# Edge and source scatters counted anew over the stages of a four-layer graph network, and one wait less for GpSimd's gathers

## The reference

```python
# layer 0, feed-forward: a shared expert and 2 of 8 routed experts
shared = gelu(x @ W1s + b1s) @ W2s + b2s
mask = ... top-2 of softmax(x @ Wr) ...
h = gelu(einsum('bsd,edf->bsef', x, W1p) + b1p)
priv = einsum('bsef,efd->bsed', h, W2p) + b2p
x = x + shared + einsum('bsed,bse->bsd', priv, mask)
# layer 1, graph: needs the 50000 x 256 edge attributes, summed by dst
msg = relu(x[src] + edge_attr)
agg = zeros_like(x).at[dst].add(msg)
# then an MLP with normalizations, then 1 of 32 experts
# layer 2, graph: needs maxima and sums by src
m = segment_max(e, src); denom = segment_sum(exp(e - m[src]), src)
```

## Time and profile before

| | |
|---|---|
| median of 3 runs | 5876.17 us (5872.45 to 5876.91) |
| profiled execution | 5874.7 us |
| its span | 5872.7 us, mean granted TensorE clock 0.832 |
| busy share | PE 76%, PEld 50%, DVE 62%, ACT 31%, POOL 61% |
| DMA | 901.08 MB, mean 153 GB/s |
| GpSimd's edge stores (L879) | 391, some 0.99 us each |
| GpSimd's source stores (L803) | 391, 384.8 us in total, mean 984 ns |

### The profile page before, as it was taken

One profiled execution on the slowest core, in us unless ns is written; L12 is line 12 of the kernel. 1 busy time (PEld: TensorE's weight loads), 2 busy tenths in 40 slices (PEclk: granted clock), 3 DMA queues, 4 the chain that ended last, 5 costly groups with the idle time before them and its releaser, 6 DMA issues. The chain is left out here.

```text
span 5872.7 us, 84688 instructions
## 1 busy us (share of the span) xinstructions
PE 4469.9 (76%) x19486; PEld 2920.1 (50%) x19486; DVE 3651.1 (62%) x12388; ACT 1837.0 (31%) x6462; POOL 3579.9 (61%) x3819
## 2 busy tenths in 40 slices
PE   4668777778867777659488866888597688878868
PEld 3333335767843334434355535666495333346636
DVE  9987643301037775533466677888524688888875
ACT  0000002222323333212423334554143455544421
POOL 3767775676657775575577756776124477756620
PEclk9985667989976567655899988999697799999978
DMA  1053336687757675023254447987374488854400
GB/s 54 25 165 102 104 105 167 218 263 240 248 153 208 206 205 127 25 77 99 68 134 126 127 87 245 286 285 230 122 211 134 131 230 233 231 139 139 144 20 22
DMA packets 526942, 901.08 MB, mean 153 GB/s; under 512 B 101137, under 2 KB 383712, under 8 KB 518016
## 3 DMA queue, kind: packets, MB, share of 16 engines
q0 software_dynamic: 164160, 449.94, 27.7%
q1 hardware_dynamic: 301866, 317.09, 17.4%
q10 hardware_dynamic: 60438, 128.64, 7.1%
HBM read 725.55 MB, written 169.76 MB: 152 GB/s over the span
## 5 line engine op out<-in xcount | busy, mean ns | idle before, releaser
L1021 PE MATMUL bank<-small 128*125 128x256 f32 x1660 | 818.7, 615 | 277.8 <-DVE small L988 173.0
L969 POOL DMA_INDIRECT small<-tabA,idxD x830 | 803.2, 968 | 275.2 <-issue 181.3
L1021 PEld LDWEIGHTS bank<-small 128*125 128x125 f32 x1660 | 373.9, 278 | 721.7 <-DVE small L988 409.8
L1554 DVE COPY small<-bank 128x256 f32<-128x256 f32 x176 | 74.7, 425 | 737.9 <-PE bank L1609 737.9
L803 POOL DMA_INDIRECT recs<-pkS,rowS x391 | 384.8, 984 | 231.3 <-issue 100.4
L2907 POOL DMA_INDIRECT small<-tabC,idxD x415 | 408.5, 984 | 190.7 <-SPq L202 64.6
L2645 POOL DMA_INDIRECT big<-tabB,idxD x415 | 396.2, 955 | 195.6 <-issue 89.6
L2432 POOL DMA_INDIRECT big<-tabT,idxS x415 | 415.8, 1002 | 139.0 <-issue 109.7
L1000 DVE TENSOR_TENSOR big<-big,bank 125x256 f32 x830 | 346.5, 417 | 231.2 <-PE bank L1021 216.2
L2985 PE MATMUL bank<-big,cst 128*125 128x512 f32 x830 | 426.7, 595 | 0.5 <-ACT big L2972 0.5
L1598 PE MATMUL bank<-small,big 128*128 128x128 f32 (+1 forms) x3040 | 413.7, 295 | 0.0
(11 more groups left out here) (484 smaller groups left out, 10370.2 us busy)
## 6 DMA issues: line engine op xcount, KB each, us to landing
small<-eaS SPq DMA_DIRECT2D x830, 128.0 KB
big<-in_L_w ACTq DMA_DIRECT2D x56, 1024.0 KB
eaS<-small SPq DMA_DIRECT2D x415, 128.0 KB, 2.8
big<-in_L2f_w ACTq DMA_DIRECT2D x64, 512.0 KB
ytab<-small ACTq DMA_DIRECT2D x176, 128.0 KB
big<-rowsS SPq DMA_DIRECT2D x52, 256.0 KB
small<-rowsD SPq DMA_DIRECT2D x52, 256.0 KB
big<-rowsD SPq DMA_DIRECT2D x52, 256.0 KB
```

The lines of the kernel that those rows point to most:

```text
L969: g.indirect_dma_start(out=self.gb[k % self.RG], out_offset=None, in_=K.tabA, in_offset=row_index(K.idxD, k)).then_inc(*self.got.up(k))
L1021: p.matmul(self.K.bank[k % 4][0:PT, 0:D], self.oh[k % self.RO][:, 0:PT], self.gb[k % self.RG], start=True, stop=True).then_inc(*self.summe ...
```

## The change

In the fused stage GpSimd and SyncE issue 5 edge pieces per step (before 6 and 7 in turn, 162 in all, now 125). In the first expert stage four edge pieces and one source piece follow each gather (before three and two), so that 199 edge pieces are stored there (before 162), until tile 51, and 54 source pieces (before 108); the two waits for `e_hid` and `e_y` are gone. In layer 1's MLP 140 source pieces are issued (before 79): two in each of 24 steps, six in each of seven chunks as before, two in each of the 25 last steps. In the scores stage there are 25 (before 50). The group stage and the second expert stage keep 19 and 54. Layer 2's projection is left with 99 (before 81), 75 in its steps and 24 (before 6) behind the last step.

```diff
@@ fused_sync
-            self.side.edges.sync(s, 7 if t % 2 else 6)
+            self.side.edges.sync(s, 5)
@@ fused_gpsimd
             self.side.edges.gpsimd(g, 3)
             if t:
                 g.wait_ge(*self.out2.n(t))
-            self.side.edges.gpsimd(g, 4 if t % 2 else 3)
+            self.side.edges.gpsimd(g, 2)
@@ expert_gpsimd
             if k >= self.RX:
                 g.wait_ge(*self.e_flip.n(k - self.RX + 1))
-            if self.shared and k >= 4:
-                g.wait_ge(*self.e_hid[1].n(k - 3))
             g.indirect_dma_start(out=self.xg[k % self.RX], out_offset=None, in_=K.tabA, in_offset=row_index(self.tix, k)).then_inc(*self.rows_in.up(k))
             if self.shared and k >= 2:
-                self.side.edges.gpsimd(g, 2)
-                if k >= 6:
-                    g.wait_ge(*self.e_y.n(k - 5))
-                self.side.edges.gpsimd(g, 1)
-                self.side.source.gpsimd(g, 2)
+                self.side.edges.gpsimd(g, 4)
+                self.side.source.gpsimd(g, 1)
@@ L1Mlp.gpsimd
-        for t in range(0, T - 1, 2):
+        for t in range(T - 1):
             if t:
                 g.wait_ge(*self.biased.n(t))
-            self.source.gpsimd(g, 1)
+            self.source.gpsimd(g, 2)
         for i in range(7):
             g.wait_ge(*self.second.n(2 * i + 1))
             self.source.gpsimd(g, 6)
         for t in range(T):
             g.wait_ge(*self.back.n(t + 1))
-            self.source.gpsimd(g, 1)
+            self.source.gpsimd(g, 2)
@@ build
-                 side=SideWork(edges, (0, 3, 0), source, (0, 2, 0)))
+                 side=SideWork(edges, (0, 4, 0), source, (0, 1, 0)))
-                 side=SideWork(None, None, source, (2, 1, 19)))
+                 side=SideWork(None, None, source, (1, 1, 19)))
```

## The result

The changed kernel takes 5893.64 us (median of 13 runs, 5878.99 to 5905.24), the kernel before 5871.14 in the same series (13 runs, 5861.85 to 5887.75): ratio 1.0040, 95% interval 1.0028 to 1.0051, so 22.5 us slower, 0.4%. The spans of the profiled executions are 5891.9 and 5872.7, 19.2 apart.

The account below looks back on a forecast made before the run. GpSimd's instruction slots and the edge ring were taken to bound the touched stages. Stage differences −51 fused, +45 first expert, +19 MLP, −21 scores, +24 layer 2 sum to +16, giving 5892 us on the median's scale, range 5858 to 5932.

Parts of the forecast that it names:

- Fused stage, −51 forecast: Fused stage: 37 fewer edge scatters at 1.29 us shorten GpSimd's tail behind TensorE; −51 us, from −46 to −56.
- First expert stage, +45 forecast: First expert stage: four edge scatters per tile make the five-buffer ring the bound, 9.44 us per tile; +45, from −43 to +82.
- The round of 11.8 us: First expert stage, one edge buffer's cycle: store landing 5.1, load landing 5.1, loaded buffer's turn on GpSimd 1.6 us.
- the prediction's sign of being wrong: First expert stage: gathers every 8.5 us or less, needing edge loads and stores landing in under 5 us beside the weights.
- Two of its other signs: First expert stage: GpSimd's waits for edge loads rise from 52 to some 130 us; TensorE waits for gathers in most tiles.
- The removed waits, 0 forecast: First expert stage: dropping the waits for `e_hid` and `e_y` is worth 0, since GpSimd is late, not ahead.
- MLP, +19 forecast: Layer 1's MLP: 61 more source scatters, of which the last steps' 50 outlast VectorE; +19 us, from +16 to +23.
- Layer 2, +24 forecast: Layer 2's projection: GpSimd is the bound, so all 18 added scatters count; +24 us, between 22.7 and 26.8.
- A: First expert stage: the ring does not bind, transfers land in 3.1 us; stage −43, whole −72, 5804 us; chance 0.06.
- B: First expert stage: the ring binds mildly, 8.6 us per tile; stage +4, whole −25, 5851 us; chance 0.18.
- C: First expert stage: the ring binds hard; stage +82, whole +53, 5929 us; chance 0.22.
- D: Fused stage: the gain falls short because the 25 steps delay scatters more; −46 at worst, chance 0.04 for 10 us or more.

Follow-up runs that it names:

- the first two experiments: Kernel before without the two waits of the first expert stage, 5879.75 us; changed kernel with both waits put back, 5892.27 us; one run each.
- the two waits alone: Kernel before with the two waits of the first expert stage (hidden layer, output) taken out, nothing else changed: 5879.75 us in one run.
- the next three: Changed kernel with the two waits put back, 5892.27 us; with eight edge buffers, 5809.39; with a quarter of the first expert stage's first-matrix bytes, 5794.95.
- the next two: Changed kernel with eight edge buffers in place of five, 5809.39 us; with a quarter of each tile's first weight matrix loaded in the first expert stage, 5794.95.
- the second run of the sources' part: Kernel before with only the changed kernel's source scatter counts, edges and waits as before, on the other chip: 6508.67 us (10 runs), ratio 0.9972.

## Why the prediction was right

The forecast was 5892 us and the median is 5893.64; the sum was +16 and the profiles differ by 19.2, the medians by 22.5. The signs of all five terms held. That the forecast and the median are 2 us apart is luck in part: the kernel before has a median of 5871.14 over 13 runs, 5 under the 5876.17 from which the forecast was counted, so the change cost 6.5 us more than was said.

*Fused stage, −51 forecast, −50.4 measured.* The 37 scatters at the tail's own pace were the right price (47.7; the other 2.7 fit the tail's wait of 6.39 for a load, which is gone), and the rest of the steps' scatters hid behind TensorE as assumed. The tail is 8 us, under the 10 named.

*First expert stage, +45 forecast, +49.9 measured.* The gathers of tiles 2 to 51 are 9.49 us apart on average (1158.20 to 1623.43, 49 intervals), 9.44 was forecast; that makes the gather of tile 51 fall 467.8 us behind the first, not 465.1. TensorE starts that tile 6.05 us later and not 4.3, and the end, 5 × 7.25 + 14.1, is as computed. The mechanism is shown by two runs: eight buffers take 66 us off with the same bytes, and a quarter of the weights' bytes takes 95 off, with no wait for an edge load left. So it was neither the fourth scatter as such nor, by the first two experiments, the removed waits.

The round of 11.8 us was right, and partly by luck. In the changed kernel's stage a buffer's load stands 6.84 us before its scatter and the next load 4.99 behind it, on average over 190 rounds: 11.83, and 9.46 per tile. The second part is the store, forecast as 5.1. The first was to be 5.1 for the load's landing and 1.6 for the turn; by the semaphore records the load landed in 4.5 and waited 2.4, near the full 2.5 of the bound. So the prediction's sign of being wrong, loads landing in under 5, was there for the loads, and the longer turn made up for it.

Two of its other signs came out weaker. GpSimd waited for loads for 105.4 us and not 130. This count has in each of its 53 waits the 0.30 that stands between any two instructions and that the slot of 1.26 holds already; without them it is 89.5, and 49 tiles of 9.44 − 7.6 are 90. The 130 did not follow from the prediction's own terms. The same 0.30 explains why its 458 us for the kernel before were 9 more than the 449.2 measured: 31 waits of 0.30 were counted twice. And TensorE does not wait in most tiles, but at 18 of them after the first, 75.6 us in all: most gaps are 3.3 to 6.9 us long, and the tiles between run at full pace.

*The removed waits, 0 forecast.* Right: −3.7 alone, and −0.5 in the changed kernel.

*MLP, +19 forecast, +14.9 measured: the size was off.* The 44 and the chunks hid as forecast (the last steps begin 126.5 us into the stage, 126.3 before). The 50 scatters took 65.0 us to the end of the last, inside the 63 to 69 of the bounds. The upper of these took a scatter beside busy VectorE for 1.146 us; with VectorE busy for 41.4 of the 45 us to 2475 (41.7 before) the median scatter took 0.958, so VectorE's work alone does not make them long, and what did before stays open. But the stage was released 3.9 us before that end, as ScalarE's row shows: GpSimd passes the meet with three scatters still queued. Without that the term would have been 18.8, so the step that was mis-sized is the end of the stage, taken as the end of the last scatter.

*Scores, −21 forecast, −20.8 measured.* VectorE goes from its last instruction of this stage to the first of the next without idle time.

*Layer 2, +24 forecast, +19.0 measured: the size was off.* The 18 added scatters cost what was forecast: from the 76th scatter to the last, the kernel before takes 6.3 us (5 intervals) and the changed one 30.7 (23), 24.4 more. But the 76th stood 107.3 us into the stage, where it stood at 112.8 before:

```profile
2908.43 0.95 POOL L803 DMA_INDIRECT recs<-pkS,rowS  x1 [0.73 <-DMA recs<-pkS,rowS]
...
2914.73 0.96 POOL L803 DMA_INDIRECT recs<-pkS,rowS  x1 [0.30 <-issue]
```

```profile
2898.71 1.03 POOL L803 DMA_INDIRECT recs<-pkS,rowS  x1 [0.30 <-issue]
...
2929.41 0.96 POOL L803 DMA_INDIRECT recs<-pkS,rowS  x1 [0.30 <-issue]
```

The scatters up to there are the same in both, and other executions on the fast chip have them at 109.6 (the two waits alone) and at 111.6, 108.9 and 109.5 (the next three). So the 5 us are the difference of one execution from another; the four traces with 99 scatters have 151.7 to 155.2 us in this stage, the two with 81 have 131.3 and 132.7.

The terms' errors, +4.9, −4.1 and −5.0 among them, nearly cancel, and that is luck too.

*The rest, +6.6.* It lies in stages that the change doesn't touch, +4.5 of it in the second edge sum (549.2 us before). That stage took +6.5 and +6.1 in the first two experiments and −1.1 and −4.0 in the next two, against the one profile of before, and nothing in the edits orders these. I take it for the difference of one execution from another; it wasn't settled.

*The rivals.* A, that the ring doesn't bind, is the changed kernel with few weights on the way: its expert stage of 431.7 was nearly met with 434.6. It did not hold with the full weights, where even eight buffers leave 463.1. B and C are out on the fast chip, where the stage is 5 us off the forecast. D, the fused gain falling short, is out with 50.4. On the other chip the loads hold GpSimd up little, and yet the whole change with six buffers is 0.34% slower; its expert stage is 546 us, with TensorE's pauses and six slots per tile, and which of them binds was not taken apart.

The best version found is the changed schedule with eight edge buffers, 0.9908 of before on the fast chip; its gain on the other is in doubt, since eight buffers gave the kernel before nothing there. The kernel before with eight buffers was not run on the fast chip, so how much of the 0.9908 is owed to the buffers alone is open.

## What to carry to other kernels

When a stream of load and scatter goes through a ring of N buffers, the time of a consumer's step is at least (pieces per step)/N of a buffer's round (here 4/5 of 11.83, 9.46, and 9.49 measured); read the landing of its transfers in the stage into which you move them, beside that stage's own loads, before you move them from an empty tail into it. Moving a fixed count of instructions from stage to stage on a bound queue pays where another engine ends the stage that receives them (the 36 added in the MLP's first product cost nothing, the 18 of layer 2 their full 24 us). Count the gain and the price in slots. Where the stage's end waits only until they are queued, leave out the last few. A few more buffers can be worth more than the order: here three more buffers turned +0.4% into −0.9%, on the chip where the ring was the bound.

## What the runs showed of the hardware

The second chip took 6452.66 and 6525.83 us for the kernel before, 10 and 11% more than the fast one. It isn't confined to the expert stage: the sort stage at the start takes 425 to 474 us there to TensorE's first instruction of the next stage, and 384.8 to 386.8 in the six traces of the fast chip, with TensorE paused for "issue" 50.0 us at one line of it:

```profile
PE bank L669 <- DVE small L630: 73.4, 63, 5.6
...
PE bank L669 <- issue: 50.0, 21, 11.9
```

(TensorE's waits in the first 448 us of the second run of the sources' part.) The same stage varies by 48 us between kernels that do the same work in it, so one profile on that chip tells stage lengths roughly. What these pauses are stays open.

GpSimd's queue reaches a meet while up to three of its indirect DMAs, 3.9 us, are still to be worked off; a profile row of a scatter can so begin after the stage that it belongs to has ended for all other engines. At the end of the changed kernel's fused stage it is two: the meet is complete at 1152.9, and scatters of that stage begin at 1153.12 and 1154.38.
